# Rotary keys: the addition and the low part on VectorE, those of the queries on POOL, with a counter for each

## The chip, the cores and the metric

One Trainium2 chip, one of its cores. The metric is the device time of one execution in microseconds (us). Engines: TensorE (PE, its weight loads PEld), VectorE (DVE), ScalarE (ACT), GpSimd (POOL), and the queue of SyncE (SP), which only issues DMAs. The engines run their own instruction lists in order and wait for each other through semaphores that count up.

## The reference

One transformer layer on x of 4 sequences x 256 tokens x 256 features, all in float32. Cut to what matters:

```
def rope(x):                                   # per head, 128 features
    rot = concatenate([-x2, x1])               # the two halves swapped, one negated
    return x * cos + rot * sin

h = layernorm(x)
q = rope(heads(h @ wq.T, 16)); k = rope(heads(h @ wk.T, 4)); v = heads(h @ wv.T, 4)
o = lightning_attn(q, repeat(k, 4), repeat(v, 4))   # (q k^T * decay mask) v, causal, no softmax
x = x + o @ wo.T
x = x + (fwht(silu(h2 @ W1.T) * (h2 @ W3.T))) @ W2.T   # h2 = layernorm(x)
```

Four query heads share one key head.

## The kernel before

**Split products.** Each float32 operand of a TensorE product is held as a high part (`*_hi`, ScalarE copies it into the fp32r type) and a low part (`*_lo` = value - high part). A product is three matmuls (`product`, L274 to L276): hi x hi, hi x lo, lo x hi.

**Tiling.** The tokens are worked on in two halves of 512 (`c` = 0, 1). In each half the 16 heads are 8 pairs, and a pair of a half is a unit: `u` = 0 to 15, `c, p = divmod(u, 8)`. Two pairs share a key head. In unit `u` TensorE computes the scores of the unit in three pieces (`scores`, pieces S_FIRST0, S_SECOND, S_FIRST1, banks 2 to 4), the rest of the attention of the unit before (`attend`), output projections (`project_out`), and as filling work the projections of unit `u` + 2: two query heads (`queries(u)`) and, where `u` is even, one key head (`key(u)`). They go to banks 0 and 1 in turn. After the 16 units the feed-forward part follows.

**Rotary step of one projected tile** `item` (128 features x 512 tokens), numbered `r` in the list ROPE; its buffers `rope_a`, `rope_b`, `qk` have two slots, `r % 2`:
1. ScalarE, `swap` (L509, L510): the two halves of the bank into `rope_b`, swapped.
2. VectorE, `rotate` (L779, L780): `rope_a` = bank x cos, which frees the bank (`lin_free`), and `rope_b` = `rope_b` x sin (`rope_parts`).
3. POOL, `rope_add` (L647): `qk` = `rope_a` + `rope_b` (`rope_sum`).
4. ScalarE, `high_rope` (L515): the high part into `k_hi` or `q_hi` (`rope_hi`). q_hi and q_lo lie in the tensor `q_hid`, which rows name.
5. POOL, `low_rope` (L654): the low part into `k_lo` or `q_lo` (`rope_lo`).

The next tile of the same slot waits in steps 1 and 2 for `rope_sum` of tile `r - 2`, in step 3 for `rope_lo` of tile `r - 2`. `scores` waits for `rope_lo` of the later one of its key and its second query.

**Order.** Every engine's list is written out by hand. The key projected in unit `u - 1` (even) takes steps 1 to 5 in unit `u` (odd), together with the rest of the two queries projected just ahead of it, and is used from unit `u` + 1 on. So the units 1, 3, 5, 7, 9, 11 and 13 are those with a key, called key units here; the eighth key, `("K", 0, 0)`, is in the start. In a key unit POOL's list was: low part of the first query of unit `u - 1`, addition of the key, low part of the second query, low part of the key, additions of the two new queries. VectorE's list in the loop: masks (`mask`, L793), `rotate` of the key, low parts of the masked scores (`low_p`, L798) and of the attention output (`low_o`, L803), third mask, `rotate` of two new queries, `low_o`, third `low_p`. `attend(u, 1)` on TensorE stands in unit `u` + 1 behind two pieces of `scores` and one `project_out`, and waits for the third `low_p`.

The high and low parts of weight chunks (L481 on ScalarE, L659 on POOL from chunk 4 on) lie between these steps.

Of the kernel before, what the change touches and what calls it, by code (L numbers as in the profile page):

```python
# [44 lines left out]
PPG = PAIRS // KVH  # L45
# [62 lines left out]
ROPE_NO = {item: n for n, item in enumerate(ROPE)}  # L108
V_NO = {item: n for n, item in enumerate(i for i in LIN if i[0] == "V")}
X_NO = {item: n for n, item in enumerate(i for i in LIN if i[0] == "X")}  # L110
FIRST_ROPE = 5


S_FIRST0, S_SECOND, S_FIRST1 = range(3)
# [5 lines left out]
def build(nc, x, wk, wv, wq, wo, w1, w3, w2, cos, sin, decay, ident, hadamard, out):  # L120
    dram = {"wk": wk, "wv": wv, "wq": wq, "wo": wo, "w1": w1, "w3": w3, "w2": w2}

    with ExitStack() as ctx:
# [3 lines left out]
        def sem(name):  # L127
            return ctx.enter_context(nc.semaphore(name))
# [62 lines left out]

        lin_full, lin_free = sem("lin_full"), sem("lin_free")
        x_hi_done, v_hi_done = sem("x_hi_done"), sem("v_hi_done")
        swapped, rope_parts, rope_sum = sem("swapped"), sem("rope_parts"), sem("rope_sum")
        rope_hi, rope_lo = sem("rope_hi"), sem("rope_lo")

        s_full, mask_done, p_hi_done = sem("s_full"), sem("mask_done"), sem("p_hi_done")
        p_lo_done = sem("p_lo_done")
# [72 lines left out]
        def _(pe):  # L271
# [46 lines left out]
            def scores(u, s):  # L318

                c, p = divmod(u, PAIRS)  # L320
                ks, qs = p // PPG % 2, p % 2
                needed = max(ROPE_NO[("Q", c, 2 * p + 1)], ROPE_NO[("K", c, p // PPG)])
                pe.wait_ge(rope_lo, needed + 1)
                if u:
                    pe.wait_ge(p_lo_done, 3 * (u - 1) + s + 1)
                if s == S_SECOND:
                    for b in range(BH):
                        a = slice(b * SEQ + P, (b + 1) * SEQ)
                        last = product(s_bank[s][:, b * 256:(b + 1) * 256], k_hi[:, ks, a], k_lo[:, ks, a],
                                       q_hi[:, qs, :, a], q_lo[:, qs, :, a], True, True)  # L330
# [143 lines left out]
        def _(act):  # L474
# [27 lines left out]
            def swap(item):  # L502

                n, r = LIN_NO[item], ROPE_NO[item]
                act.wait_ge(lin_full, n + 1)
                if r >= 2:
                    act.wait_ge(rope_sum, r - 1)
                h = P // 2
                act.activation(rope_b[0:h, r % 2, :], lin_bank(n)[h:P], ACT.Copy)  # L509
                act.activation(rope_b[h:P, r % 2, :], lin_bank(n)[0:h], ACT.Copy).then_inc(swapped, 1)  # L510

            def high_rope(item):
                r = ROPE_NO[item]
                act.wait_ge(rope_sum, r + 1)
                act.activation(rope_dst(item)[0], qk[:, r % 2, :], ACT.Copy).then_inc(rope_hi, 1)  # L515

            def high_p(u, s):
# [118 lines left out]
        @block.gpsimd  # L636
        def _(pool):
            def inverse_deviation(i):
                pool.wait_ge(eps_done, i + 1)
                pool.tensor_tensor(rstd[:], var_eps[:], minus_half[:], ALU.pow).then_inc(rstd_done, 1)  # L640

            def rope_add(item):
                r = ROPE_NO[item]
                pool.wait_ge(rope_parts, r + 1)
                if r >= 2:
                    pool.wait_ge(rope_lo, r - 1)
                pool.tensor_tensor(qk[:, r % 2, :], rope_a[:, r % 2, :], rope_b[:, r % 2, :],  # L647
                                   ALU.add).then_inc(rope_sum, 1)

            def low_rope(item):  # L650
                r = ROPE_NO[item]
                hi, lo = rope_dst(item)
                pool.wait_ge(rope_hi, r + 1)
                pool.tensor_tensor(lo, qk[:, r % 2, :], hi.bitcast(F32), ALU.subtract).then_inc(rope_lo, 1)  # L654

            def low_weights(n):
                _, _, at = CHUNKS[n]
                pool.wait_ge(w_hi_done, n + 1)
                pool.tensor_tensor(w_lo[:, at:at + CH], w_raw[:, n % SLOTS, :], w_hi[:, at:at + CH].bitcast(F32),  # L659
                                   ALU.subtract).then_inc(w_lo_pool, 1)  # L660

            def butterfly(dc, step):

                n = CHUNK_NO[("w2", dc)]
                if step:
                    pool.wait_ge(fly_done, 3 * dc + step)
                else:
                    pool.wait_ge(w_loaded[n % SLOTS], 16 * (n // SLOTS + 1))
                    if dc:
                        pool.wait_ge(w2_lo_done, dc)  # L670
                    else:
                        pool.wait_ge(lin_full, LIN_NO[("X", 2, KD - 1)] + 1)
                src, dst = w_raw[:, n % SLOTS, :], xn_flat
                if step == 1:
                    src, dst = dst, src
                s, d = (a.rearrange("p (m two r) -> p m two r", m=1 << step, two=2) for a in (src, dst))
                pool.tensor_tensor(d[:, :, 0, :], s[:, :, 0, :], s[:, :, 1, :], ALU.add)
                pool.tensor_tensor(d[:, :, 1, :], s[:, :, 0, :], s[:, :, 1, :], ALU.subtract).then_inc(fly_done, 1)

            pool.memset(minus_half[:], -0.5).then_inc(half_set, 1)  # L680
            pool.wait_ge(half_set, 1)
            inverse_deviation(0)
            rope_add(("K", 0, 0))
            rope_add(("Q", 0, 0))
            low_rope(("K", 0, 0))
            rope_add(("Q", 0, 1))
            low_rope(("Q", 0, 0))
            low_rope(("Q", 0, 1))
            rope_add(("Q", 0, 2))
            rope_add(("Q", 0, 3))  # L690
            low_rope(("Q", 0, 2))
            low_rope(("Q", 0, 3))
            low_weights(4)
            for u in range(UNITS):
                if u:
                    before = queries(u - 1)
                    for item in before[:1]:
                        low_rope(item)
                    if u % PAIRS == 3:
                        inverse_deviation(u // PAIRS + 1)  # L700
                    for item in key(u - 1):
                        rope_add(item)
                    for item in before[1:] + key(u - 1):
                        low_rope(item)
                for item in queries(u):
                    rope_add(item)
                if unit_chunk(u) is not None:
                    low_weights(unit_chunk(u))
                if u >= UNITS - 2:
                    for step in range(3):  # L710
                        butterfly(u - UNITS + 2, step)
            inverse_deviation(3)

        @block.vector
        def _(dve):
# [54 lines left out]
            def rotate(item):  # L770

                n, r = LIN_NO[item], ROPE_NO[item]
                dve.wait_ge(swapped, r + 1)
                if r >= 2:
                    dve.wait_ge(rope_sum, r - 1)
                src, a, b = (m.rearrange("p (b t) -> p b t", b=BH)
                             for m in (lin_bank(n)[:], rope_a[:, r % 2, :], rope_b[:, r % 2, :]))
                c, s = (tb[:].unsqueeze(1).broadcast_to([P, BH, SEQ]) for tb in (cos_sb, sin_sb))
                dve.tensor_tensor(a, src, c, ALU.mult).then_inc(lin_free, 1)  # L779
                dve.tensor_tensor(b, b, s, ALU.mult).then_inc(rope_parts, 1)  # L780

            def mask(u, s):
                c, p = divmod(u, PAIRS)
# [87 lines left out]
            for u in range(UNITS):  # L871
                if u:
                    mask(u, S_FIRST0)
                    mask(u, S_SECOND)
                    fill(key(u - 1) + turned(u - 1))
                    low_p(u, S_FIRST0)
                    low_o(u - 1, 1)
                    low_p(u, S_SECOND)
                fill(values(u)[:1])
                mask(u, S_FIRST1)  # L880
                if u == PAIRS + 1:
                    add_attention(0, 1)
# [104 lines left out]
```

## Time and profile before

| | |
|---|---|
| median of 3 runs | 277.31 us (277.09 to 278.17) |
| profiled execution, its time | 277.34 us |
| profiled execution, span from first to last instruction | 275.5 us |
| granted TensorE clock | 1.0 of full speed |
| busy: PE, DVE, ACT, POOL | 257.6, 206.1, 167.1, 153.2 us |

The span is 1.8 us shorter than the execution's time; the rest lies around it. Busy time of PE is the union of matmuls whose ends are modelled. A row of a timeline gives start, duration, engine, line, operation and tiles; a bracket behind it gives the idle time before it and who ended that. Instructions of VectorE overlap a little in these rows: one of 0.68 us is followed by the next 0.60 us after its start.

### The profile page before, as it was taken

The page shows a single profiled execution, that of the slowest core. Times are in us where ns is not written, and L with a number is a line of the kernel's source. Part 1 is how long each engine was busy: PE and PEld are TensorE (multiplying, and loading weights), DVE is VectorE, ACT ScalarE, POOL GpSimd, SP SyncE. Part 2 cuts the span into 40 slices and gives each one's busy share as a digit, 9 for nine tenths or more (in the row PEclk, how much of TensorE's full clock was granted, in tenths as well). Part 3 has the DMA queues.
Part 4 walks back from the last instruction along what each step waited for, and adds up shares of the span by engine and source line. Part 5 has one row for each costly group of instructions (what it writes and reads, how often), then busy time and mean ns, then how long its engine had stood idle before and what let it go on. Part 6 is the DMA issues. An engine that isn't in the chain of part 4 may idle for free.

```text
span 275.5 us, 4150 instructions
## 1 busy us (share of the span) xinstructions
PE 257.6 (93%) x1480; PEld 225.1 (82%) x1480; DVE 206.1 (75%) x324; ACT 167.1 (61%) x279; POOL 153.2 (56%) x111
## 2 busy tenths in 40 slices
PE   0796878999999999999999999999999999999995
PEld 0584766898898988878888888898989879988895
DVE  2878799899997988967999898795756985144433
ACT  2586787678689767655667777995352552043230
POOL 1049989978878935813597787899709400000000
PEclk9999999999999999999999999999999999999999
DMA  7695022102022000000002002200000000200002
GB/s 259 242 355 190 0 80 77 59 20 76 4 76 76 0 2 0 1 4 0 0 2 76 2 0 76 76 4 1 2 0 0 2 0 0 79 0 0 2 0 76
DMA packets 5203, 13.23 MB, mean 48 GB/s; under 512 B 576, under 2 KB 2112, under 8 KB 5184
## 3 DMA queue, kind: packets, MB, share of 16 engines
q1 hardware_dynamic: 4752, 12.65, 13.0%
q10 hardware_dynamic: 432, 0.33, 0.4%
q8 instruction: 12, 0.20, 0.3%
q14 instruction: 7, 0.06, 0.1%
HBM read 11.93 MB, written 1.05 MB: 47 GB/s over the span
## 4 chain that ended last, share of the span: by engine, by line
PE 70%; DVE 13%; POOL 5%; issue 5%; ACT 3%; DMA 3%; SPq 0%; DVEq 0%; POOLq 0%
PE bank L274 24%; PE bank L275 23%; PE bank L276 23%; DVE rope_b L780 3%; POOL qk L647 2%; POOL q_hid L654 2%; DVE rope_a L779 2%; DMA w_raw<-in_wq 1%; DMA x_sb<-in_x 1%; PE bank L287 1%; DVE xn L748 1%; DVE rope_b L817 1%; DVE w_lo L754 1%; POOL w_lo L659 1%; DVE p_lo L798 1%
## 5 line engine op out<-in xcount | busy, mean ns | idle before, releaser
L647 POOL TENSOR_TENSOR qk<-rope_a,rope_b 128x512 f32<-128x512 f32 x40 | 53.5, 1341 | 34.8 <-DVE rope_b L780 34.4
L274 PE MATMUL bank<-xt_hi,w_hi 128*128 128x512 f32 x144 | 57.4, 398 | 1.5 <-DVE rope_a L779 0.8
L275 PE MATMUL bank<-xt_lo,w_hi 128*128 128x512 f32 x144 | 56.9, 395 | 0.0
L276 PE MATMUL bank<-xt_hi,w_lo 128*128 128x512 f32 x144 | 56.6, 393 | 0.0
L654 POOL TENSOR_TENSOR q_hid<-qk,q_hid 128x512 fp32r<-128x512 f32 x32 | 43.0, 1355 | 9.7 <-ACT q_hid L515 9.7
L780 DVE TENSOR_TENSOR rope_b<-rope_b,sin_sb 128x512 f32<-128x512 f32 x40 | 42.1, 1053 | 0.0
L522 ACT ACTIVATE p_hi<-bank 128x512 fp32r<-128x512 f32 x48 | 28.6, 596 | 15.7 <-DVE bank L793 15.2
L779 DVE TENSOR_TENSOR rope_a<-bank,cos_sb 128x512 f32<-128x512 f32 x40 | 27.5, 686 | 14.2 <-ACT rope_b L510 13.5
L275 PE MATMUL bank<-w_lo,o_hi 128*128 128x256 f32 x128 | 36.2, 283 | 0.0
L276 PE MATMUL bank<-w_hi,o_lo 128*128 128x256 f32 x128 | 36.2, 283 | 0.0
L274 PE MATMUL bank<-w_hi,o_hi 128*128 128x256 f32 x128 | 36.1, 282 | 0.0
L274 PEld LDWEIGHTS bank<-xt_hi,w_hi 128*128 128x128 f32 x144 | 27.6, 191 | 8.0 <-DVE rope_a L779 1.0
L798 DVE TENSOR_TENSOR p_lo<-bank,p_hi 128x512 fp32r<-128x512 f32 x48 | 32.7, 680 | 1.4 <-ACT p_hi L522 1.0
L276 PEld LDWEIGHTS bank<-xt_hi,w_lo 128*128 128x128 f32 x144 | 27.5, 191 | 5.9
L793 DVE TENSOR_TENSOR bank<-bank,decay_sb 128x512 f32<-128x512 f32 x48 | 32.0, 688 | 0.5
L275 PEld LDWEIGHTS bank<-xt_lo,w_hi 128*128 128x128 f32 x144 | 27.5, 191 | 5.1
L509 ACT ACTIVATE rope_b<-bank 64x512 f32<-64x512 f32 x40 | 23.8, 596 | 11.8 <-PE bank L276 11.0
L533 ACT ACTIVATE rope_a<-bank 128x512 f32<-128x512 f32 x16 | 9.5, 596 | 28.5 <-PE bank L276 28.5
L803 DVE TENSOR_TENSOR o_lo<-bank,o_hi 128x512 fp32r<-128x512 f32 x32 | 22.0, 687 | 5.9 <-ACT o_hi L526 5.4
L817 DVE TENSOR_TENSOR rope_b<-bank,rope_a 128x512 f32<-128x512 f32 x16 | 11.0, 689 | 20.6 <-ACT rope_a L533 20.6
L526 ACT ACTIVATE o_hi<-bank 128x512 fp32r<-128x512 f32 x32 | 19.1, 596 | 12.1 <-PE bank L276 11.4
L275 PEld LDWEIGHTS bank<-w_lo,o_hi 128*128 128x128 f32 x128 | 24.5, 191 | 0.7
(72 smaller groups left out, 591.4 us busy)
## 6 DMA issues: line engine op xcount, KB each, us to landing
w_raw<-in_w SPq DMA_DIRECT2D x6, 512.0 KB, 3.3
w_raw<-in_wq SPq DMA_DIRECT2D x4, 512.0 KB, 4.8
decay_sb<-in_decay SPq DMA_DIRECT2D x4, 512.0 KB, 6.3
w_raw<-in_wo SPq DMA_DIRECT2D x4, 512.0 KB, 3.2
x_sb<-in_x SPq DMA_DIRECT2D x4, 256.0 KB, 4.5
out<-x_sb SPq DMA_DIRECT2D x8, 128.0 KB, 1.8
w_raw<-in_wk SPq DMA_DIRECT2D x1, 512.0 KB, 4.7
w_raw<-in_wv SPq DMA_DIRECT2D x1, 512.0 KB, 6.6
```

Of the source, the lines that this page charges most:

```text
L274: pe.matmul(o, a_hi, b_hi, start=first, stop=False, skip_group_check=shared)
L275: pe.matmul(o, a_hi, b_lo, start=False, stop=False, skip_group_check=shared)
L276: return pe.matmul(o, a_lo, b_hi, start=False, stop=last, skip_group_check=shared)
L509: act.activation(rope_b[0:h, r % 2, :], lin_bank(n)[h:P], ACT.Copy)
L522: act.activation(p_hi[:, s, :], s_bank[s][:], ACT.Copy).then_inc(p_hi_done, 1)
L647: pool.tensor_tensor(qk[:, r % 2, :], rope_a[:, r % 2, :], rope_b[:, r % 2, :], ALU.add).then_inc(rope_sum, 1)
L654: pool.tensor_tensor(lo, qk[:, r % 2, :], hi.bitcast(F32), ALU.subtract).then_inc(rope_lo, 1)
L779: dve.tensor_tensor(a, src, c, ALU.mult).then_inc(lin_free, 1)
L780: dve.tensor_tensor(b, b, s, ALU.mult).then_inc(rope_parts, 1)
L793: dve.tensor_tensor(src, src, table, ALU.mult).then_inc(mask_done, 1)
L798: dve.tensor_tensor(p_lo[:, s, :], s_bank[s][:], p_hi[:, s, :].bitcast(F32), ALU.subtract).then_inc(p_lo_done, 1)
L803: dve.tensor_tensor(o_lo[:, b, :, :].rearrange("p h t -> p (h t)"), o_bank[:], o_hi[:, b, :, :].rearrange("p h t -> p (h t)").bitcast(F32) ...
```

## The change

The addition and the low part of a key tile move from POOL to VectorE (`key_add`, `low_key`); those of the query tiles stay on POOL. `rope_sum` and `rope_lo`, which counted all tiles, become four counters: `key_sum`, `key_lo` (counted up by VectorE), `query_sum`, `query_lo` (by POOL). Who waited for tile `r` now waits for the counter of its kind. `scores` waits for its key and its query apart. Eight keys are concerned. ScalarE's list, TensorE's matmuls and the DMAs are unchanged. (`FIRST_ROPE`, a name that nothing used, is dropped.)

```diff
+        def wait_rope_sum(engine, r):
+            item = ROPE[r]
+            if item[0] == "K":
+                engine.wait_ge(key_sum, KEY_NO[item] + 1)
+            else:
+                engine.wait_ge(query_sum, QUERY_NO[item] + 1)
...
-                needed = max(ROPE_NO[("Q", c, 2 * p + 1)], ROPE_NO[("K", c, p // PPG)])
-                pe.wait_ge(rope_lo, needed + 1)
+                wait_rope_low(pe, ROPE_NO[("K", c, p // PPG)])
+                wait_rope_low(pe, ROPE_NO[("Q", c, 2 * p + 1)])
...
-            rope_add(("K", 0, 0))
             rope_add(("Q", 0, 0))
-            low_rope(("K", 0, 0))
...
-                    for item in key(u - 1):
-                        rope_add(item)
-                    for item in before[1:] + key(u - 1):
+                    for item in before[1:]:
                         low_rope(item)
...
+            def key_add(item):
+                r = ROPE_NO[item]
+                dve.wait_ge(rope_parts, r + 1)
+                if r >= 2:
+                    wait_rope_low(dve, r - 2)
+                dve.tensor_tensor(qk[:, r % 2, :], rope_a[:, r % 2, :], rope_b[:, r % 2, :],
+                                  ALU.add).then_inc(key_sum, 1)
+
+            def low_key(item):
+                r = ROPE_NO[item]
+                hi, lo = rope_dst(item)
+                dve.wait_ge(rope_hi, r + 1)
+                dve.tensor_tensor(lo, qk[:, r % 2, :], hi.bitcast(F32), ALU.subtract).then_inc(key_lo, 1)
...
-            fill(START[2:5])
+            rotate(("K", 0, 0))
+            key_add(("K", 0, 0))
+            fill(START[3:5])
+            low_key(("K", 0, 0))
             low_weights(3)
...
                     low_p(u, S_SECOND)
+                    for item in key(u - 1):
+                        key_add(item)
                 fill(values(u)[:1])
                 mask(u, S_FIRST1)
...
-                fill(values(u)[1:2] + queries(u))
+                fill(values(u)[1:2] + queries(u)[:1])
+                for item in key(u - 1) if u else []:
+                    low_key(item)
+                fill(queries(u)[1:])
```

POOL's list in unit 1, before (L647 addition, L654 low part, L659 low part of weights):

```order
L647 TENSOR_TENSOR qk<-rope_a,rope_b 128x512 [waits rope_lo,rope_parts] x2
L659 TENSOR_TENSOR w_lo<-w_raw,w_hi 128x1024 [waits w_hi_done]
L654 TENSOR_TENSOR q_hid<-qk,q_hid 128x512 [waits rope_hi]
L647 TENSOR_TENSOR qk<-rope_a,rope_b 128x512 [waits rope_lo,rope_parts]
L654 TENSOR_TENSOR q_hid<-qk,q_hid 128x512 [waits rope_hi]
L654 TENSOR_TENSOR k_lo<-qk,k_hi 128x512 [waits rope_hi]
L647 TENSOR_TENSOR qk<-rope_a,rope_b 128x512 [waits rope_lo,rope_parts] x2
```

The same place now, where L665 is the addition, L672 the low part and L677 that of weights:

```order
L665 TENSOR_TENSOR qk<-rope_a,rope_b 128x512 [waits query_lo,rope_parts] x2
L677 TENSOR_TENSOR w_lo<-w_raw,w_hi 128x1024 [waits w_hi_done]
L672 TENSOR_TENSOR q_hid<-qk,q_hid 128x512 [waits rope_hi] x2
L665 TENSOR_TENSOR qk<-rope_a,rope_b 128x512 [waits query_lo,rope_parts]
L665 TENSOR_TENSOR qk<-rope_a,rope_b 128x512 [waits key_lo,rope_parts]
```

Two instructions of the key are gone, the two low parts of the queries stand together, and the second new query's addition waits for VectorE's `key_lo`.

VectorE's list in unit 1, before, from `rotate` of the key on (L779, L780 rotate, L793 mask, L798 `low_p`, L803 `low_o`):

```order
L779 TENSOR_TENSOR rope_a<-bank1,cos_sb 128x512
L780 TENSOR_TENSOR rope_b<-rope_b,sin_sb 128x512
L798 TENSOR_TENSOR p_lo<-bank2,p_hi 128x512
L803 TENSOR_TENSOR o_lo<-bank5,o_hi 128x512
L798 TENSOR_TENSOR p_lo<-bank3,p_hi 128x512
L793 TENSOR_TENSOR bank4<-bank4,decay_sb 128x512
L779 TENSOR_TENSOR rope_a<-bank0,cos_sb 128x512
L780 TENSOR_TENSOR rope_b<-rope_b,sin_sb 128x512
L779 TENSOR_TENSOR rope_a<-bank1,cos_sb 128x512
L780 TENSOR_TENSOR rope_b<-rope_b,sin_sb 128x512
```

The same place now (L793, L794 rotate, L821 mask, L826 `low_p`, L831 `low_o`, L801 `key_add`, L808 `low_key`):

```order
L793 TENSOR_TENSOR rope_a<-bank1,cos_sb 128x512
L794 TENSOR_TENSOR rope_b<-rope_b,sin_sb 128x512
L826 TENSOR_TENSOR p_lo<-bank2,p_hi 128x512
L831 TENSOR_TENSOR o_lo<-bank5,o_hi 128x512
L826 TENSOR_TENSOR p_lo<-bank3,p_hi 128x512
L801 TENSOR_TENSOR qk<-rope_a,rope_b 128x512
L821 TENSOR_TENSOR bank4<-bank4,decay_sb 128x512
L793 TENSOR_TENSOR rope_a<-bank0,cos_sb 128x512
L794 TENSOR_TENSOR rope_b<-rope_b,sin_sb 128x512
L808 TENSOR_TENSOR k_lo<-qk,k_hi 128x512
L793 TENSOR_TENSOR rope_a<-bank1,cos_sb 128x512
L794 TENSOR_TENSOR rope_b<-rope_b,sin_sb 128x512
```

The key's addition stands in front of the third mask, its low part between the two new queries.

## Rows read from the trace of the kernel before

**Rows 1.** The page, busy time of the engines (share of the span), instructions.
```profile
PE 257.6 (93%) x1480; PEld 225.1 (82%) x1480; DVE 206.1 (75%) x324; ACT 167.1 (61%) x279; POOL 153.2 (56%) x111
```

**Rows 2.** Waits of PE, whole span: us in total, times, longest.
```profile
PE bank L274 <- DVE v_hid L766: 2.3, 1, 2.3
PE bank L274 <- DVE p_lo L798: 1.8, 2, 1.4
PE bank L274 <- POOL k_lo L654: 1.3, 1, 1.3
```

**Rows 3.** Groups by line and shape: count, busy, mean ns, idle before and releaser.
```profile
L647 POOL TENSOR_TENSOR qk<-rope_a,rope_b 128x512 f32<-128x512 f32 x40 | 53.5, 1341 | 34.8 <-DVE rope_b L780 34.4
L780 DVE TENSOR_TENSOR rope_b<-rope_b,sin_sb 128x512 f32<-128x512 f32 x40 | 42.1, 1053 | 0.0
...
L654 POOL TENSOR_TENSOR k_lo<-qk,k_hi 128x512 fp32r<-128x512 f32 x8 | 14.0, 1748 | 3.6 <-ACT k_hi L515 3.6
```

**Rows 4.** Timeline of PE, unit 1 to 2: attend's last, first of scores, next attend.
```profile
45.97 0.28 PE L276 MATMUL bank<-p_hi,v_hid 128*128 128x256 f32 x1
47.59 0.50 PE L274 MATMUL bank<-q_hid,k_hi 128*128 128x512 f32 x1 [1.34 <-POOL k_lo L654]
...
50.55 0.40 PE L274 MATMUL bank<-p_hi,v_hid 128*128 128x512 f32 x1
```

**Rows 5.** Timeline of DVE, unit 1, from the third mask to the third low_p.
```profile
43.73 0.68 DVE L793 TENSOR_TENSOR bank<-bank,decay_sb 128x512 f32<-128x512 f32 x1
...
44.93 1.49 DVE L780 TENSOR_TENSOR rope_b<-rope_b,sin_sb 128x512 f32<-128x512 f32 x1
...
47.13 0.95 DVE L780 TENSOR_TENSOR rope_b<-rope_b,sin_sb 128x512 f32<-128x512 f32 x1
...
48.61 0.68 DVE L798 TENSOR_TENSOR p_lo<-bank,p_hi 128x512 fp32r<-128x512 f32 x1
```

**Rows 6.** Timeline of POOL, unit 1: key addition, second query's low part, key's low part.
```profile
43.30 1.30 POOL L647 TENSOR_TENSOR qk<-rope_a,rope_b 128x512 f32<-128x512 f32 x1
44.55 1.31 POOL L654 TENSOR_TENSOR q_hid<-qk,q_hid 128x512 fp32r<-128x512 f32 x1
45.82 1.72 POOL L654 TENSOR_TENSOR k_lo<-qk,k_hi 128x512 fp32r<-128x512 f32 x1
```

**Rows 7.** Timelines of the start: three rows of DVE, then one of POOL.
```profile
17.62 1.40 DVE L780 TENSOR_TENSOR rope_b<-rope_b,sin_sb 128x512 f32<-128x512 f32 x1
...
19.55 1.93 DVE L754 TENSOR_TENSOR w_lo<-w_raw,w_hi 128x1024 fp32r<-128x1024 f32 x1
...
22.00 1.18 DVE L780 TENSOR_TENSOR rope_b<-rope_b,sin_sb 128x512 f32<-128x512 f32 x1
...
19.10 1.29 POOL L647 TENSOR_TENSOR qk<-rope_a,rope_b 128x512 f32<-128x512 f32 x1 [0.63 <-DVE rope_b L780]
```

**Rows 8.** Timelines of unit 3: three rows of DVE, then PE's attend(3, 1).
```profile
67.36 1.51 DVE L780 TENSOR_TENSOR rope_b<-rope_b,sin_sb 128x512 f32<-128x512 f32 x1
...
69.40 1.41 DVE L780 TENSOR_TENSOR rope_b<-rope_b,sin_sb 128x512 f32<-128x512 f32 x1
...
71.33 0.68 DVE L798 TENSOR_TENSOR p_lo<-bank,p_hi 128x512 fp32r<-128x512 f32 x1
...
72.06 0.50 PE L274 MATMUL bank<-p_hi,v_hid 128*128 128x512 f32 x1 [0.39 <-DVE p_lo L798]
```

**Rows 9.** Timelines: PE's scores and attend in units 11 and 12; POOL in 11.
```profile
150.80 0.39 PE L274 MATMUL bank<-q_hid,k_hi 128*128 128x512 f32 x1
...
153.63 0.40 PE L274 MATMUL bank<-p_hi,v_hid 128*128 128x512 f32 x1
...
160.66 0.50 PE L274 MATMUL bank<-q_hid,k_hi 128*128 128x512 f32 x1
...
163.66 0.50 PE L274 MATMUL bank<-p_hi,v_hid 128*128 128x512 f32 x1
...
158.87 1.74 POOL L654 TENSOR_TENSOR k_lo<-qk,k_hi 128x512 fp32r<-128x512 f32 x1 [0.69 <-ACT k_hi L515]
```

More of the change, by code:

```diff
@@ L110 @@
 X_NO = {item: n for n, item in enumerate(i for i in LIN if i[0] == "X")}
-FIRST_ROPE = 5
+KEY_NO = {item: n for n, item in enumerate(i for i in ROPE if i[0] == "K")}
+QUERY_NO = {item: n for n, item in enumerate(i for i in ROPE if i[0] == "Q")}
 S_FIRST0, S_SECOND, S_FIRST1 = range(3)
@@ L193, in build @@
         x_hi_done, v_hi_done = sem("x_hi_done"), sem("v_hi_done")
-        swapped, rope_parts, rope_sum = sem("swapped"), sem("rope_parts"), sem("rope_sum")
-        rope_hi, rope_lo = sem("rope_hi"), sem("rope_lo")
+        swapped, rope_parts, rope_hi = sem("swapped"), sem("rope_parts"), sem("rope_hi")
+        key_sum, key_lo = sem("key_sum"), sem("key_lo")
+        query_sum, query_lo = sem("query_sum"), sem("query_lo")
         s_full, mask_done, p_hi_done = sem("s_full"), sem("mask_done"), sem("p_hi_done")
@@ L215, in wait_low_weights, with wait_rope_low @@
                 engine.wait_ge(w_lo_pool, n + 1 - LOW_ON_DVE)
+        def wait_rope_sum(engine, r):
[4 more added lines that the diff above has]
+                engine.wait_ge(query_sum, QUERY_NO[item] + 1)
+        def wait_rope_low(engine, r):
+            item = ROPE[r]
+            if item[0] == "K":
+                engine.wait_ge(key_lo, KEY_NO[item] + 1)
+            else:
+                engine.wait_ge(query_lo, QUERY_NO[item] + 1)
         def lin_bank(n):
@@ L506, in swap @@
                 if r >= 2:
-                    act.wait_ge(rope_sum, r - 1)
+                    wait_rope_sum(act, r - 2)
                 h = P // 2
@@ L513, in high_rope @@
                 r = ROPE_NO[item]
-                act.wait_ge(rope_sum, r + 1)
+                wait_rope_sum(act, r)
                 act.activation(rope_dst(item)[0], qk[:, r % 2, :], ACT.Copy).then_inc(rope_hi, 1)
@@ L645, in rope_add @@
                 if r >= 2:
-                    pool.wait_ge(rope_lo, r - 1)
+                    wait_rope_low(pool, r - 2)
                 pool.tensor_tensor(qk[:, r % 2, :], rope_a[:, r % 2, :], rope_b[:, r % 2, :],
-                                   ALU.add).then_inc(rope_sum, 1)
+                                   ALU.add).then_inc(query_sum, 1)
             def low_rope(item):
@@ L653, in low_rope @@
                 pool.wait_ge(rope_hi, r + 1)
-                pool.tensor_tensor(lo, qk[:, r % 2, :], hi.bitcast(F32), ALU.subtract).then_inc(rope_lo, 1)
+                pool.tensor_tensor(lo, qk[:, r % 2, :], hi.bitcast(F32), ALU.subtract).then_inc(query_lo, 1)
             def low_weights(n):
@@ L774, in rotate @@
                 if r >= 2:
-                    dve.wait_ge(rope_sum, r - 1)
+                    wait_rope_sum(dve, r - 2)
                 src, a, b = (m.rearrange("p (b t) -> p b t", b=BH)
```

## The prediction

> **What bounds the kernel now.** I read the busy times first: PE 257.6 of 275.5 us, 93%, next DVE 75%, POOL 56% [rows 1]. PE is the bound, so the change is worth what it adds to or takes from PE's gaps, nothing else. Then PE's own waits: inside the attention part they are few: 2.3 us once on a low part of a value tile in the start, 1.8 us in two waits for `low_p`, 1.3 us once on POOL's `k_lo` [rows 2]. Only the last is a key's. The timelines add waits too short for that view. From the first matmul of `scores` to `attend` a free-running PE needs 153.63 - 150.80 = 2.83 us; in unit 12 it takes 163.66 - 160.66 = 3.00 us, with a first matmul of 0.50 instead of 0.39 us at both ends, and the first starts just after POOL's `k_lo` ends at 158.87 + 1.74 = 160.61 [rows 9]. The traces of units 8 and 10 repeat this to 0.02 us.
>
> **What an instruction of the rotary step costs.** POOL needs about 1.3 us for one of 128x512 [rows 6], mean 1.34 [rows 3]. VectorE needs 0.68 us, the next starts 0.60 us after it. But L780, VectorE's product with two operands in SBUF, has a mean of 1053 ns, and POOL's `k_lo` one of 1748 [rows 3]. The rows show why: VectorE's L780 of 44.93 lasts 1.49 us and ends at 46.42, 0.60 us after POOL's instruction of 44.55 ended at 45.82 + 0.04; POOL's next, 45.82, then lasts 1.72 and ends at 47.54, which is 46.3 + 1.25; VectorE's L780 of 47.13 ends at 48.08, again 0.6 behind it [rows 5, 6]. So a VectorE instruction with two SBUF operands and a POOL instruction run one behind the other, the one that waits goes first, and instructions that read a bank (masks, `low_p`, `rope_a`) don't take part: the mask of 43.73 takes 0.68 beside POOL's addition [rows 5, 6]. Both added instructions of VectorE have two SBUF operands. I price each at 0.60 us plus what is left of the POOL instruction that runs as it arrives.
>
> A rule speaks against the change here. The Trainium skill ("Perfetto Trace Analysis", Optimizing Scalar/DVE Operations) says that moving operations between GPSIMD and DVE might not help, because they share an SBUF read port. By it the whole difference would be about 0 us; the rows above show the sharing, and by them the difference is small too, but made of a loss and a gain.
>
> **The change part by part.**
>
> *Start.* Before, VectorE's L780 of the first query stood from 17.62 for 1.40 us behind POOL's key addition, and `w_lo` from 19.55 for 1.93 us behind POOL's query addition of 19.10 [rows 7]. Now `key_add` takes 17.1 to 17.8 (some 0.1 for its wait on its own engine's last result), L780 of the query meets no POOL and ends at 19.0 as before (17.62 + 1.40 = 19.02). `low_key` comes at 19.55, waits out POOL's addition (19.10 + 1.29 = 20.39), ends at 21.0; `w_lo` starts at 21.0, ends at 22.1 instead of 21.48. The next L780 starts 0.6 us later, at 22.6, but no longer stands behind POOL's `k_lo`: it ends at 23.3, before at 22.00 + 1.18 = 23.18 [rows 7]. From there all is as before, 0.1 us later, and with it the 2.3 us wait of PE [rows 2]. **+0.1 us.**
>
> *Unit 1, the key's low part.* POOL now does the second query's low part at once, 43.12 to 44.4, where the key's addition stood [rows 6]. `key_add` comes at 43.73, waits for it, and runs 44.4 to 45.1. The mask, `rope_a` and L780 follow at 0.60 us each, to 46.9, and `low_key` ends at 47.5 (ScalarE has 1.7 us for `k_hi`, 0.63 us of work). Before, `k_lo` ended at 47.54 and PE went on at 47.59 [rows 4, 6]. So the 1.34 us wait stays as it is: POOL's chain is replaced by a VectorE chain of the same length. **0.**
>
> *Unit 1, what stands behind it on VectorE.* All from the third mask on is later. L780 of the second new query comes at 48.0, POOL's addition of the first one now holds 47.5 to 48.7 (it could start at 46.95 but comes behind `low_key`), so it ends at 49.3, and `low_p` goes 49.9 to 50.5; before 48.61 to 49.28 [rows 5]. `attend` started at 50.55 [rows 4] with 1.2 us of slack and now has none: it starts at about 50.6 and its first matmul has the 0.1 us of a restart. **+0.15 us.** In unit 2 VectorE gets the delay back in its own waits for ScalarE.
>
> *Unit 3.* VectorE is without a pause here. It gets two instructions, 1.2 us, and L780 of 67.36 (1.51 us) loses its POOL neighbour, 0.83 us; L780 of 69.40 (1.41 us) keeps one [rows 8]. Net +0.35 us on the third `low_p`, which ends at 71.33 + 0.68 = 72.01 and for which PE already waits 0.39 us [rows 8]. That goes straight into PE. **+0.3 us.**
>
> *Units 5 and 13.* The same lateness of about 1.3 us as in unit 1 arises, but the timeline leaves `attend` 1.3 us there as well. **0, with nothing to spare.**
>
> *Units 7, 9, 11.* Here VectorE pauses for ScalarE before each `rotate`, which takes up `key_add` and `low_key`. In unit 11 POOL's `k_lo` of 158.87 had a 0.44 us wait for VectorE in it and ended at 160.61 [rows 9]; `low_key` follows L780 of the first query at 159.4 and ends at 160.05, so `scores` starts unhindered. POOL's next addition then moves up by 0.5 us, and so do the last L780 and `low_p`. The two short waits go: 3.00 - 2.83 = 0.17 us, some 0.08 us of waiting ahead of it, and the 0.11 us by which the second first matmul is slow (0.50 against 0.39): 0.36 us. Unit 7 is alike. In unit 9 an addition to x (L810) stands between and uses up most, 0.1 us is left. **-0.8 us.**
>
> *POOL loses* 16 instructions, some 53.5 / 40 x 8 + 14.0 = 24.7 us of recorded time [rows 3], none of it on PE's path but for the waits named. The counters cost nothing: the waits are made in the engines' queues ahead of instructions.
>
> Sum: 0.1 + 0.15 + 0.3 - 0.8 = -0.25. Against the profiled execution's own 277.34 us that is **277.1 us**; the median of the runs, 277.31, is the same to 0.03 us.
>
> **The rivals.**
>
> *POOL gets in first (slower).* `low_key` and POOL's addition of the first new query are released by the same L780: VectorE goes on 0.08 us before that ends in the rows (0.60 against 0.68), POOL begins 0.08 us after (19.10 against 17.62 + 1.40 = 19.02 [rows 7]). If POOL wins this 0.16 us, `low_key` is 1.25 us later in each of the 7 key units, and `scores` waits for it with hardly any slack: about 1.1 us each, +7.7, **284.8 us**. It decides from the point where VectorE's wait on `rope_hi` costs over 0.16 us. For it speaks only how near the two lie. Against it: in all meetings of the trace the one that was there first goes first, and VectorE is in possession. The Trainium skill ("SBUF — State Buffer", Who interferes with whom) has the same as issue order deciding who blocks for the whole instruction; that makes this a question of 0.16 us as well, and moves no number.
>
> *VectorE is full in the first half (slower).* If `key_add` and `low_key` save nothing by POOL's missing instructions, unit 3 costs 1.2 instead of 0.3, unit 1 has 0.6 more, unit 5 0.3, and the gain of 0.9 in 7, 9 and 11 doesn't come: +2.7, **279.8 us**. For it: VectorE works without pause from about 55 to 74. Against it: L780 with a mean of 1053 ns against 680 undisturbed [rows 3] shows how much of its time is waiting for POOL.
>
> *The key's chain becomes short (faster).* If `key_add` slips in at 43.73, ahead of POOL's second low part, `low_key` ends at 46.8 and 0.75 us of the 1.34 goes [rows 4]; the same in unit 3 takes away 0.3 of mine and PE's 0.5 there, to **275.5 us**. Against it: POOL goes from one instruction to the next without a pause (43.30 + 1.30 against 44.55 [rows 6]).
>
> **How the numbers follow.** Forecast 0.66: the pieces are worked out to some 0.1 us each, but there are eight keys, and the units with no slack may give 0.5 us more. POOL first 0.12, VectorE full 0.13, short chain 0.09. The range of 8 in 10 takes in the forecast and the second and third rival, not POOL first: 275.6 to 280.2. A measurement of this kernel tells 0.5% (1.4 us) from no change, so the borders are 275.9 and 278.7. Faster: the short chain with the edge of the forecast, 0.09. Slower: the two slower rivals less the part of the second that stays below 278.7, and an edge of the forecast, 0.22. Same: 0.69.
>
> **What would show it.** POOL's list shrinks by 16 instructions and its `k_lo` rows vanish; VectorE gets 16 of 0.7 to 1.3 us, L780's mean falls from 1053 toward 950 ns. Start: PE's wait for the value tile again 2.3 us. Unit 1: `scores` waits some 1.3 us for `k_lo` of VectorE. Unit 3: PE waits 0.7 us for `low_p`. Units 8, 10, 12: 2.83 us from `scores` to `attend`. I am wrong if `low_key` lasts about 1.9 us in the key units, which is POOL first; or if PE's waits for `low_p` pile up in unit 5 or 13.

## The result and the profile after

| | before | changed |
|---|---|---|
| median (range) of 20 runs each | 277.33 us (276.81 to 278.38) | 278.0 us (277.54 to 279.19) |
| profiled span | 275.5 us | 276.5 us |
| busy: PE, DVE, ACT, POOL | 257.6, 206.1, 167.1, 153.2 us | 257.0, 211.1, 166.6, 131.7 us |

The ratio is 1.0026 (95% interval 1.0017 to 1.0036): the changed kernel is slower by 0.7 us. The forecast was 277.1 us, a gain of 0.25 us. The time lies in its range and within 0.5% of before, but the sign was wrong.

The page of the changed kernel, busy times (against [rows 1]) and the groups of the rotary step (against [rows 3]; L665 is POOL's addition, L794 the former L780):

```profile
PE 257.0 (93%) x1480; PEld 224.8 (81%) x1480; DVE 211.1 (76%) x340; ACT 166.6 (60%) x279; POOL 131.7 (48%) x95
...
L665 POOL TENSOR_TENSOR qk<-rope_a,rope_b 128x512 f32<-128x512 f32 x32 | 44.5, 1393 | 59.1 <-DVE rope_b L794 59.1
...
L794 DVE TENSOR_TENSOR rope_b<-rope_b,sin_sb 128x512 f32<-128x512 f32 x40 | 36.8, 919 | 0.0
```

POOL does 16 instructions less and is busy for 21.5 us less. VectorE does 16 more and is busy for only 5.0 us more, in the main because its products with two SBUF operands wait less for POOL: mean 919 instead of 1053 ns, 5.3 us over the 40 of them.

PE's waits in the changed kernel (against [rows 2]):

```profile
PE bank L292 <- DVE v_hid L780: 2.5, 1, 2.5
PE bank L292 <- DVE k_lo L808: 1.7, 2, 1.2
PE bank L292 <- DVE p_lo L826: 1.4, 1, 1.4
PE bank L305 <- DVE rope_a L793: 1.0, 2, 0.5
```

Three lines are of the kind that stood there before. The last is new: L305 is the transpose, two waits of 0.5 us for `rope_a`.

**The lag, unit by unit.** Since PE does the same 1480 matmuls in the same order, the start of each in the two traces can be subtracted. The lag of the changed kernel was 0.28 us at 14.4 us, before any key was worked on (the first loads came later), so the two profiled executions lie 0.96 us apart (278.3 against 277.34 us) where the medians lie 0.7 us apart. From there it moved in steps:

| stretch | lag before -> behind, us | step | step forecast |
|---|---|---|---|
| start | 0.28 -> 0.43 | +0.15 | +0.1 |
| unit 1 | 0.43 -> 0.30 | -0.13 | +0.15 |
| unit 3 | 0.30 -> 0.46 | +0.16 | +0.3 |
| unit 5 | 0.46 -> 1.18 | **+0.72** | 0 |
| unit 7 | 1.18 -> 0.79 | -0.39 | -0.36 |
| unit 9 | 0.79 -> 0.48 | -0.31 | -0.1 |
| unit 11 | 0.48 -> 0.15 | -0.33 | -0.36 |
| unit 13 | 0.15 -> 0.87 | **+0.72** | 0 |
| rest | 0.87 -> 0.93 | +0.06 | 0 |

Two units carry the loss. Without them the steps add up to a gain of 0.8 us. The steps repeat in the other runs that move the same keys, to some 0.05 us: -0.1 in unit 1, +0.1 to +0.2 in unit 3, -0.4, -0.3 and -0.35 in units 7, 9 and 11. Only the step of the start does not: it hangs on when PE comes to its wait for the value tile, which differs between the executions by up to 1.6 us. The timelines of unit 5 show how. Before, VectorE and then PE (L287 is the transpose; `x8` is both turned tiles in one go):

```profile
88.06 0.68 DVE L779 TENSOR_TENSOR rope_a<-bank,cos_sb 128x512 f32<-128x512 f32 x1
88.66 1.13 DVE L780 TENSOR_TENSOR rope_b<-rope_b,sin_sb 128x512 f32<-128x512 f32 x1
89.91 0.69 DVE L779 TENSOR_TENSOR rope_a<-bank,cos_sb 128x512 f32<-128x512 f32 x1
...
90.31 1.03 PE L287 MATMUL bank<-ident_sb,xn 128*128 128x128 f32 x8
```

The same in the changed kernel, from `key_add` on:

```profile
87.92 0.89 DVE L801 TENSOR_TENSOR qk<-rope_a,rope_b 128x512 f32<-128x512 f32 x1
88.73 0.69 DVE L821 TENSOR_TENSOR bank<-bank,decay_sb 128x512 f32<-128x512 f32 x1
89.33 0.67 DVE L793 TENSOR_TENSOR rope_a<-bank,cos_sb 128x512 f32<-128x512 f32 x1
89.93 0.67 DVE L794 TENSOR_TENSOR rope_b<-rope_b,sin_sb 128x512 f32<-128x512 f32 x1
90.53 0.68 DVE L808 TENSOR_TENSOR k_lo<-qk,k_hi 128x512 fp32r<-128x512 f32 x1
91.13 0.68 DVE L793 TENSOR_TENSOR rope_a<-bank,cos_sb 128x512 f32<-128x512 f32 x1
...
90.75 0.60 PE L305 MATMUL bank<-ident_sb,xn 128*128 128x128 f32 x4
91.86 0.66 PE L305 MATMUL bank<-ident_sb,xn 128*128 128x128 f32 x4 [0.51 <-DVE rope_a L793]
92.28 0.47 PE L292 MATMUL bank<-q_hid,k_hi 128*128 128x512 f32 x1
```

In units 5 and 13 PE transposes the normalised tokens of the next half (`turned`) as the last thing of the unit, into banks 0 and 1. Bank 1 is freed by `rope_a` of the second new query. Before, that ended at 90.60, and the transposes of the second tile (the last four of the eight) started at 90.75, with 0.15 us to spare; now it ends at 91.81, and they start at 91.86.

### The profile page after: what moved, and what is told of

The parts are those of the page before. It is cut to its first block, busy times and chain, and to the rows that moved or that the text cites. A ratio compares the mean times of both kernels' runs of the same rounds, so it can differ in the third digit from the quotient of the medians.

```text
span 276.5 us, 4153 instructions
## 1 busy us (share of the span) xinstructions
PE 257.0 (93%) x1480; PEld 224.8 (81%) x1480; DVE 211.1 (76%) x340; ACT 166.6 (60%) x279; POOL 131.7 (48%) x95
## 4 chain that ended last, share of the span: by engine, by line
PE 63%; DVE 18%; ACT 7%; issue 6%; DMA 3%; POOL 2%; SPq 0%; DVEq 0%; ACTq 0%; POOLq 0%
PE bank L292 21%; PE bank L293 20%; PE bank L294 20%; DVE rope_b L794 3%; DVE rope_a L793 2%; DVE bank L821 2%; DVE qk L801 2%; ACT xn L511 1%; ACT w_hi L499 1%; DMA x_sb<-in_x 1%; DMA w_raw<-in_wq 1%; DVE k_lo L808 1%; DVE p_lo L826 1%; DVE xn L762 1%; POOL qk L665 1%
## 5 line engine op out<-in xcount | busy, mean ns | idle before, releaser
L665 POOL TENSOR_TENSOR qk<-rope_a,rope_b 128x512 f32<-128x512 f32 x32 | 44.5, 1393 | 59.1 <-DVE rope_b L794 59.1
L672 POOL TENSOR_TENSOR q_hid<-qk,q_hid 128x512 fp32r<-128x512 f32 x32 | 43.7, 1382 | 10.1 <-ACT q_hid L533 10.1
L794 DVE TENSOR_TENSOR rope_b<-rope_b,sin_sb 128x512 f32<-128x512 f32 x40 | 36.8, 919 | 0.0
L793 DVE TENSOR_TENSOR rope_a<-bank,cos_sb 128x512 f32<-128x512 f32 x40 | 27.4, 684 | 10.1 <-ACT rope_b L528 9.6
L826 DVE TENSOR_TENSOR p_lo<-bank,p_hi 128x512 fp32r<-128x512 f32 x48 | 32.6, 680 | 1.4 <-ACT p_hi L540 0.9
L821 DVE TENSOR_TENSOR bank<-bank,decay_sb 128x512 f32<-128x512 f32 x48 | 32.0, 688 | 0.5
L831 DVE TENSOR_TENSOR o_lo<-bank,o_hi 128x512 fp32r<-128x512 f32 x32 | 22.0, 687 | 5.4 <-ACT o_hi L544 4.8
L292 PEld LDWEIGHTS bank<-w_hi,o_hi 128*128 128x128 f32 x128 | 24.5, 191 | 0.7
```

Of the source, the lines that this page charges most:

```text
L292: pe.matmul(o, a_hi, b_hi, start=first, stop=False, skip_group_check=shared)
L821: dve.tensor_tensor(src, src, table, ALU.mult).then_inc(mask_done, 1)
L826: dve.tensor_tensor(p_lo[:, s, :], s_bank[s][:], p_hi[:, s, :].bitcast(F32), ALU.subtract).then_inc(p_lo_done, 1)
L831: dve.tensor_tensor(o_lo[:, b, :, :].rearrange("p h t -> p (h t)"), o_bank[:], o_hi[:, b, :, :].rearrange("p h t -> p (h t)").bitcast(F32) ...
```

## Experiments

All versions with some keys on POOL were made with the same edit: a list of keys `DVE_KEYS` for VectorE; the others keep POOL's list and order of before and count in POOL's counters. Where the key of the start is among them, its three places are also set back to what they were.

```diff
-            if item[0] == "K":
+            if item in DVE_KEYS:
                 engine.wait_ge(key_sum, KEY_NO[item] + 1)
...
-                    for item in before[1:]:
+                    for item in pool_key(u - 1):
+                        rope_add(item)
+                    for item in before[1:] + pool_key(u - 1):
                         low_rope(item)
...
-                    for item in key(u - 1):
+                    for item in dve_key(u - 1):
                         key_add(item)
```

| keys on VectorE | median, us | before beside it, us | ratio (95%) |
|---|---|---|---|
| all (the change) | 278.0 | 277.33 | 1.0026 (1.0017 to 1.0036) |
| all but 5, 13 | 276.54 | 277.57 | 0.9963 (0.9949 to 0.9977) |
| 5, 13 only | 278.96 | 277.57 | 1.005 (1.0034 to 1.0066) |
| 7, 9, 11 only | 276.48 | 277.4 | 0.9968 (0.9956 to 0.9979) |
| start, 1, 3 only | 277.49 | 277.29 | 1.0005 (0.9992 to 1.0018) |
| 1, 7, 9, 11 only | 276.25 | 277.4 | 0.9964 (0.995 to 0.9978) |
| the same again | 276.1 | 277.29 | 0.9953 (0.9936 to 0.9969) |

### Keys of units 5 and 13 back on POOL

> The changed kernel, but the keys of units 5 and 13 are added and split on POOL again, as before the change (their waits go to POOL's counter). Theory: the changed kernel loses its time in units 5 and 13, where the turned tiles of the next half (the transposes) wait for bank 1, which rope_a of the second new query frees only after low_key; in the traces the lag behind the kernel before grows by 0.7 us at each of the two. So 1.4 us come back and the gains of units 7, 9 and 11 stay: 0.7 us under the kernel before, ratio 0.9975. Rival 1: any key on VectorE fills it up, and the gains of single units are chance of one trace: the time scales with the keys moved, 6 of 8 of +0.7 us, ratio 1.002. Rival 2: the four counters or the extra waits cost the time: ratio 1.0026 as for the change.

Ratio 0.9963. The version is faster than before, by 1.0 us where 0.7 was expected (0.9975 lies at the end of the interval), and both rivals (a cost that grows with every key, a cost of the counters) are out: six keys and all four counters are in it. PE's wait for `rope_a` at the transposes is not in its trace, and the lag does not move between 73 and 112 us.

### Only the keys of units 5 and 13 on VectorE

> The counterpart: only the keys of units 5 and 13 on VectorE, all others on POOL as before. Theory of the transposes: +0.7 us at each, nothing else: 1.4 us over the kernel before, ratio 1.005, and the trace shows two waits of PE of 0.5 us at the transposes, for rope_a. Rival 1 (VectorE fills up with every key): a quarter of the +0.7 us, ratio 1.001. Rival 2 (counters): 1.0026.

Ratio 1.005, as expected, +1.4 us. Its waits of PE are those of the kernel before to 0.2 us, and one line more:

```profile
PE bank L316 <- DVE rope_a L808: 1.0, 2, 0.5
```

The lag steps by +0.7 us twice, at the transposes of units 5 and 13 (90.8 and 182.3 us in the trace before), and by under 0.1 us anywhere else.

### `rope_a` ahead of `low_key` in units 5 and 13

```diff
                 dve.tensor_tensor(a, src, c, ALU.mult).then_inc(lin_free, 1)
+                for k in between:          # the key, in units 5 and 13
+                    low_key(k)
                 dve.tensor_tensor(b, b, s, ALU.mult).then_inc(rope_parts, 1)
```

> The changed kernel, but in units 5 and 13 low_key stands between the two instructions of the second new query's rotate: rope_a, which frees bank 1, comes 0.6 us sooner, low_key 0.6 us later. If the bank is what PE waits for there, its wait shrinks from 0.5 us to some 0.1 (ScalarE's swap of that query ends at 90.70 and is the next thing to be late), and k_lo is ready at 91.8, just ahead of scores: 0.4 us less at each of the two, 0.8 us under the changed kernel, ratio to the kernel before 0.9998. If it is k_lo or the third low_p that holds PE there, nothing is won or 0.6 us more is lost: ratio 1.0026 to 1.007.

Ratio 1.0041 (1.0027 to 1.0056): no gain over the changed kernel, in the range of the second outcome. PE's lag steps by 1.06 us in each of the two units instead of 0.7. The wait at the transposes shrank to 0.13 us, as the first outcome had it, but one for `k_lo` came. VectorE, POOL and PE in unit 5:

```profile
90.38 0.69 DVE L793 TENSOR_TENSOR rope_a<-bank,cos_sb 128x512 f32<-128x512 f32 x1
90.99 1.17 DVE L810 TENSOR_TENSOR k_lo<-qk,k_hi 128x512 fp32r<-128x512 f32 x1
...
90.34 1.27 POOL L665 TENSOR_TENSOR qk<-rope_a,rope_b 128x512 f32<-128x512 f32 x1 [2.42 <-DVE rope_b L796]
...
92.22 0.50 PE L292 MATMUL bank<-q_hid,k_hi 128*128 128x512 f32 x1 [0.43 <-DVE k_lo L810]
```

Ordered behind `rope_a`, `low_key` finds POOL's addition (started 90.34) ahead of it, lasts 1.17 instead of 0.68 us and ends at 92.16. So the bank is the first of two deadlines that lie within half a microsecond: without waits, PE makes the second four transposes in 0.44 us and goes on to the scores. (In the changed kernel `k_lo` was ready at 91.21, ahead of the scores at 92.28; it is the reordering that made it late.)

### Transposes behind the first scores

```diff
                 if u < UNITS:
                     scores(u, S_FIRST0)
                     scores(u, S_SECOND)
+                    fill(turned(u - 1) if u else [])
...
-                    fill(values(u)[3:] + key(u) + turned(u))
+                    fill(values(u)[3:] + key(u))
```

> The changed kernel, but TensorE makes the transposes for the next half behind the first two pieces of scores of unit 6 and 14 instead of ahead of them, so the wait for bank 1 has 1.5 us of other work over it. If the bank is all that holds PE there, both waits of 0.5 us go: 1.2 us under the changed kernel, ratio to the kernel before 0.998. If the whole string on VectorE is late (the run with rope_a moved forward got a wait for k_lo in its place), PE waits some 0.4 us for k_lo at scores instead: ratio 1.001 to 1.0026.

277.63 us beside 277.29, ratio 1.0004 (0.9994 to 1.0014): the time of the kernel before, with all eight keys on VectorE. PE gives the bank 1.5 us of cover and waits for nothing there, but comes to the scores before the key is ready, in unit 6 and in unit 14 alike:

```profile
90.88 0.50 PE L292 MATMUL bank<-q_hid,k_hi 128*128 128x512 f32 x1 [0.35 <-DVE k_lo L809]
...
182.02 0.50 PE L292 MATMUL bank<-q_hid,k_hi 128*128 128x512 f32 x1 [0.35 <-DVE k_lo L809]
```

This is the wait of the second stated outcome (0.35 us for `k_lo` in place of 0.5 us for the bank), though the ratio lies below the 1.001 to 1.0026 stated for it, between the two outcomes. PE's lag still steps by 0.6 us in each of the two units. The whole VectorE string is late there, not one instruction of it.

### Half the change: the addition on VectorE, the low part on POOL

```diff
-            low_key(("K", 0, 0))
...
-                for item in key(u - 1) if u else []:
-                    low_key(item)
...
+            low_rope(("K", 0, 0))
...
-                    for item in before[1:]:
+                    for item in before[1:] + key(u - 1):
                         low_rope(item)
```

All low parts are POOL's again, so they share one counter: `wait_rope_low` waits for `query_lo` to reach `r + 1`.

> Half the change: the key's addition on VectorE in all eight cases, its low part on POOL behind the second query's, as before. In units 5 and 13 rope_a of the second new query then comes 0.6 us sooner than in the changed kernel; ScalarE's swap, held up by the key's sum, ends some 0.45 us later than before the change, so PE's wait at the transposes is 0.1 to 0.2 us instead of 0.5, and POOL's low part of the key ends near 91.0 to 91.5. If low_key in front of that rope_a is the costly part of the change: 0.5 us less at each of the two, ratio to the kernel before about 0.999. If the addition is, through ScalarE's swap or through the third mask, the ratio stays at 1.0026 or above.

280.2 us beside 277.4, ratio 1.0102 (1.0089 to 1.0116): much slower than the whole change. Rows of unit 5, POOL, VectorE, PE:

```profile
89.86 1.29 POOL L668 TENSOR_TENSOR k_lo<-qk,k_hi 128x512 fp32r<-128x512 f32 x1 [1.29 <-ACT k_hi L529]
91.78 1.27 POOL L661 TENSOR_TENSOR qk<-rope_a,rope_b 128x512 f32<-128x512 f32 x1 [0.63 <-DVE rope_b L791]
...
90.24 1.46 DVE L791 TENSOR_TENSOR rope_b<-rope_b,sin_sb 128x512 f32<-128x512 f32 x1
91.62 0.68 DVE L790 TENSOR_TENSOR rope_a<-bank,cos_sb 128x512 f32<-128x512 f32 x1
92.23 1.38 DVE L791 TENSOR_TENSOR rope_b<-rope_b,sin_sb 128x512 f32<-128x512 f32 x1
...
92.36 0.66 PE L301 MATMUL bank<-ident_sb,xn 128*128 128x128 f32 x4 [0.70 <-DVE rope_a L790]
```

POOL's `k_lo` of 1.29 us now begins just ahead of L791 and holds it for 0.8 us; POOL's addition then holds the next one. In the changed kernel the same low part takes VectorE 0.60 us and holds none of its own instructions; POOL's addition waits for it. The rest of the loss is not in unit 5 alone: PE's lag steps by 0.3 us in unit 1, 0.6 in unit 3, 0.2 in unit 9 and 0.9 in units 5 and 13. So once the addition is on VectorE, the low part beside it is worth 2.1 us; I had suspected it of being the costly half. The low part on VectorE without the addition was not run.

### Keys of units 7, 9 and 11 alone, of the start, 1 and 3 alone, and of 1, 7, 9 and 11

> Only the keys of units 7, 9 and 11 on VectorE, all others on POOL. The gain of these three by itself: the lag of PE falls by 0.35 us in each, 1.05 us in all, ratio 0.9962. The forecast's own step had 0.8 us (0.36, 0.1, 0.36): 0.997. If the gain had only given back what the first half lost (PE earlier again because VectorE's lateness was caught up), it is about 0 here: ratio 1.0.

> The keys of the start and of units 1 and 3 on VectorE, all others on POOL: what the two groups run so far (7, 9, 11 and 5, 13) leave over. If the keys add up, the change's +0.7 us is -0.9 (7, 9, 11) + 1.4 (5, 13) + 0.2 (these three): ratio 1.0005, between 0.999 and 1.002. The lag of PE in the traces says start +0.15, unit 1 -0.15, unit 3 +0.2. If the first half is where VectorE being full costs the time, ratio 1.003 or above.

> Keys of units 1, 7, 9 and 11 on VectorE, those of the start and of 3, 5 and 13 on POOL. By the lag of PE in the traces a key on VectorE is worth -0.15 us in unit 1, +0.2 in unit 3, +0.1 in the start, -0.35 in each of 7, 9 and 11. If these add up: 1.2 us under the kernel before, ratio 0.9957, and 0.3 us under the version with 5 and 13 on POOL. If keys don't add up (what a key gains is taken by the next wait), the ratio stays at that version's 0.9963 or above.

> The version with the keys of units 1, 7, 9 and 11 on VectorE once more, beside other runs, since its interval was wide: ratio 0.996, and between 0.995 and 0.997 if it is really faster than the kernel before by over 0.3%.

Ratios 0.9968, 1.0005, 0.9964 and 0.9953. The three disjoint groups give -0.9, +0.15 and +1.4 us; their sum, +0.65, is the +0.7 of the change, though each of the three has an interval of 0.3 to 0.45 us to either side. The gain of 7, 9 and 11 stands without any loss ahead of it, so it is not a lost time given back. The key of unit 1 adds no more than the intervals can tell; by PE's lag it is worth 0.1 us. The version with 1, 7, 9 and 11 has the lowest medians, 276.25 and 276.1 us, but its intervals overlap those of 7, 9 and 11 alone and of all but 5 and 13.

### POOL first: pricing a rival

```diff
             def low_key(item):
                 r = ROPE_NO[item]
                 hi, lo = rope_dst(item)
+                if r:                      # second run: only the key of unit 1
+                    wait_rope_sum(dve, r + 1)
                 dve.wait_ge(rope_hi, r + 1)
```

> The changed kernel, but in every key unit low_key also waits until POOL has added the first new query, so POOL always gets in first. This prices the rival of the prediction that had POOL winning the 0.16 us: low_key some 1.3 us later in 7 units. As priced there, 1.1 us each over the changed kernel: +7.7 us, ratio to the kernel before 1.03. If part of it is hidden (units 7, 9 and 11 have some 0.5 us of slack now, and in 5 and 13 PE waits already) it is about 5 us, ratio 1.02.

290.5 us (288.8 to 292.12), ratio 1.045 (1.0413 to 1.0487): about 12 us over the changed kernel where 7.7 was priced, and outside both stated outcomes. PE's first such wait, and stretches of its trace (us; busy time of PE, PEld, DVE, ACT, POOL; then the granted clock, DMA share, GB/s):

```profile
49.01 0.50 PE L292 MATMUL bank<-q_hid,k_hi 128*128 128x512 f32 x1 [2.66 <-DVE k_lo L810]
```

```profile
44.00:49.00 5.00, 2.35 (x17) 2.01 (x16) 3.63 (x6) 3.81 (x7) 1.80 (x2) 1.00 0.06 25
49.00:53.00 4.00, 3.99 (x18) 3.81 (x19) 4.00 (x8) 0.91 (x3) 2.76 (x2) 0.57 0.00 0
53.00:70.00 17.00, 17.00 (x100) 15.05 (x100) 14.66 (x26) 11.67 (x21) 11.89 (x9) 1.00 0.20 63
...
98.00:101.00 3.00, 3.00 (x13) 2.71 (x13) 1.77 (x4) 1.66 (x4) 2.50 (x2) 0.53 0.00 0
...
196.00:200.00 4.00, 4.00 (x20) 3.82 (x20) 3.54 (x7) 2.23 (x4) 4.00 (x3) 0.57 0.00 0
```

The granted clock fell to about half (0.53 to 0.57 of full, nearly all of the stretch at 1.2 instead of 2.4 GHz) three times, each time within 1.1 us behind a long wait: 2.66 us in unit 1 and 1.99 us at the transposes of units 5 and 13. A wait of 1.94 us for the key of unit 3 was not followed by it. One place alone was run to see whether that is part of the price:

> The changed kernel, but low_key waits for POOL's addition of the first new query in unit 1 alone (in the run that had this in all key units PE waited 2.66 us there and its granted clock was 0.57 in the 4 us behind). If the wait itself is the price: 1.3 us over the changed kernel, ratio to the kernel before 1.007. If the clock behind it is part of the price, 1.5 us come on top: ratio 1.0125, and the trace shows a clock well under 1 for some 3 us behind 49 us.

280.83 us beside 277.4, ratio 1.0119 (1.0102 to 1.0137). That is 2.6 us more than the changed kernel's +0.7, and not 1.3. The lag of PE grows by 1.4 us at the wait and by another 1.5 us while the clock is low:

```profile
49.00:52.00 3.00, 3.00 (x16) 2.87 (x17) 3.00 (x7) 0.50 (x1) 1.82 (x2) 0.70 0.00 0
```

So here a wait of 2.7 us in the place of one of 1.2 cost twice what it lasted longer.

## Why the prediction was wrong in its sign

**Right.** The bound and the pricing of an instruction held, and the replay of the lists came close. `key_add` in unit 1 was to wait out POOL's low part, and `low_key` to go ahead of POOL's addition. VectorE and POOL in unit 1 of the changed kernel (against [rows 5, 6]), then PE (against [rows 4]):

```profile
44.15 1.24 DVE L801 TENSOR_TENSOR qk<-rope_a,rope_b 128x512 f32<-128x512 f32 x1
...
47.11 0.68 DVE L808 TENSOR_TENSOR k_lo<-qk,k_hi 128x512 fp32r<-128x512 f32 x1
...
50.02 0.67 DVE L826 TENSOR_TENSOR p_lo<-bank,p_hi 128x512 fp32r<-128x512 f32 x1
...
47.27 1.67 POOL L665 TENSOR_TENSOR qk<-rope_a,rope_b 128x512 f32<-128x512 f32 x1 [2.43 <-DVE rope_b L794]
...
47.84 0.50 PE L292 MATMUL bank<-q_hid,k_hi 128*128 128x512 f32 x1 [1.18 <-DVE k_lo L808]
```

Once the 0.43 us of lag that the trace had there is taken off, `key_add` ends at 44.96 (forecast 45.1), `low_key` at 47.36 (47.5) and `low_p` at 50.26 (50.5): 0.14, 0.14 and 0.24 us ahead of the forecast. POOL's addition takes 1.67 us: it came second and waited for `low_key`. The start is right: VectorE needs 9.29 us from its first `rope_a` to the third value tile's low part instead of 9.19, and 9.29 to 9.32 us in every run with both steps of that key on VectorE, 9.17 to 9.22 in every other. Unit 3 (+0.16 for +0.3) and units 7 and 11 (-0.39 and -0.33 for -0.36 each) are right in sign and nearly in size; unit 9 gave -0.31 for -0.1.

**Unit 1** came out with the other sign, -0.13 for +0.15. PE's wait for the key became 0.16 us shorter, where I had it unchanged. The slack of `attend` is used up as forecast (`low_p` ends at 50.69, `attend` starts at 50.79), but its first matmul lasts 0.45 us, 0.05 us more than before and not 0.1, and it waits for nothing.

**Unit 3** has its wait in another place than forecast: PE waits for `k_lo`, and hardly for `low_p` (against [rows 8]).

```profile
68.89 0.68 DVE L808 TENSOR_TENSOR k_lo<-qk,k_hi 128x512 fp32r<-128x512 f32 x1
70.09 1.19 DVE L794 TENSOR_TENSOR rope_b<-rope_b,sin_sb 128x512 f32<-128x512 f32 x1
...
69.62 0.50 PE L292 MATMUL bank<-q_hid,k_hi 128*128 128x512 f32 x1 [0.47 <-DVE k_lo L808]
72.57 0.46 PE L292 MATMUL bank<-p_hi,v_hid 128*128 128x512 f32 x1
```

The third `low_p` comes 0.48 us later than before, 0.3 of it lag of the trace, where +0.35 was forecast. The sum was saved because the two waits overlap: what PE loses at `scores` it does not lose again at `attend`.

**Unit 11** lost both short waits (against [rows 9]): `scores` begins with a matmul of 0.40 us and `attend` follows after 163.92 - 161.07 = 2.85 us instead of 3.00.

```profile
161.07 0.40 PE L292 MATMUL bank<-q_hid,k_hi 128*128 128x512 f32 x1
...
163.92 0.40 PE L292 MATMUL bank<-p_hi,v_hid 128*128 128x512 f32 x1
```

**The step that failed** is "Units 5 and 13": "The same lateness of about 1.3 us as in unit 1 arises, but the timeline leaves `attend` 1.3 us there as well. 0, with nothing to spare." The slack of `attend` was there (before, `low_p` ended at 92.70 and `attend` started at 94.03), and PE did not wait for `low_p` in the changed kernel. But I followed only one of those who wait for VectorE in these units, the third `low_p`. The `lin_free` count that the same string raises through `rope_a` I did not follow at all, and these are the only two key units where PE asks, within the same unit, for the bank that the second new query's `rope_a` frees. There the slack was 0.15 us. `rope_a` started 1.22 us later (91.13 against 89.91), 0.46 of it lag of the trace, so 0.76 us of its own. The lateness was thus smaller than the 1.3 us that I had (0.94 us of its own at the third `low_p`, 93.42 against 92.02), and still too much for this waiter. It cost 2 x 0.7 us where I had 0. That it is this string is shown by the two counterparts (0.9963 without, 1.005 with it alone); that it is not the bank alone by the two versions that relieved it and got `k_lo` next. My sign of being wrong looked at `low_p` in units 5 and 13, and so would have missed it too.

**The rivals.** "VectorE is full in the first half" named unit 5 but at 0.3 us, and had units 7 to 11 gain nothing: the group runs contradict it (7, 9 and 11 alone gain 0.9 us, the start, 1 and 3 alone change nothing that the interval can tell). Its own sum takes 0.9 us off for units 7 to 11 where the forecast has 0.8. "POOL gets in first" did not occur: in all seven key units `low_key` starts 0.16 us ahead of POOL's addition and lasts 0.68 us, and the addition lasts 1.66 to 1.69 us for it. Its price, 7.7 us, was too low by some 4 to 5, nearly all of which is the three stretches of low clock, about 1.5 us each. "The key's chain becomes short" did not occur: `key_add` was held by POOL's low part and took 1.24 us. Its 275.5 us also lies just outside the range that was said to take it in.

## What to carry to other kernels

When work moves to a fuller engine, list for each place everyone who waits for that engine's later results: each semaphore that it raises behind the insertion, and the next consumer of each. A check of one of them is no check: here the one that was checked had 1.3 us of slack, and the one that was not had 0.15. And where the same move is made at several places, decide it place by place: here three of eight gave 0.9 us, two cost 1.4, and the uniform version had a loss where a selective one gains 0.3 to 0.5%.

## What the runs showed of the hardware

- **Two-operand instructions of VectorE and POOL's.** The one that comes first runs undisturbed and the other waits for its end, even where they come within 0.2 us. `low_key` of 47.11 ran undisturbed (0.68 us) though POOL's addition was released by the end of the instruction ahead of it, 47.19, and started at 47.27; POOL's lasted 1.67 us instead of 1.30. The Trainium skill ("SBUF — State Buffer", Who interferes with whom) says that a VectorE instruction with two SBUF inputs contends with a GpSimd instruction that reads SBUF, and that the order of issue decides which of them blocks; these rows agree. Fewer instructions of POOL leave VectorE's undisturbed: 16 instructions more cost VectorE 5.0 us of busy time, not the 10.9 of 16 x 0.68.
- **The granted clock after a wait.** PE's wait of 2.66 us at 49 us was followed by 3 to 4 us at nearly half the clock and 1.5 us of extra time; waits of 1.2 to 1.4 us in the same place never were. The length alone does not tell: two waits of 1.99 us among the transposes were followed by a low clock, one of 1.94 us ahead of the scores of unit 4 and one of 2.46 us in the start of the changed kernel were not. What decides between them no run here shows. I had priced waits by their length alone.
- **A low clock is not always paid for.** In the version with 7, 9 and 11, the clock was low behind the start's wait of 2.72 us:

```profile
27.60:30.80 3.20, 3.15 (x12) 2.80 (x12) 2.06 (x4) 1.94 (x4) 3.20 (x3) 0.53 0.00 0
```

The lag of PE rose to 1.47 us at 29.25 and was back at 0.13 us at 39.0: before the change PE has two waits for VectorE there (0.8 us for `rope_a` and 1.4 us for `low_p`), and coming late it lost the first and had only 1.2 us of the second.
